# Sums of state products by accumulating DMAs: every second unit of the first level, and the second level, on one Trainium2 core

## The reference

```
xz = conv1x1(groupnorm(x)); x1, z = split(xz)            # 128 channels each
f1 = conv1x1(x1)           # 32x32 = 1024 positions      (level 1)
f2 = conv2x2_stride2(f1)   # 16x16 =  256 positions      (level 2)
f3 = conv2x2_stride2(f2)   #  8x8  =   64 positions      (level 3)

def ssm(x, ...):           # x: 128 channels, L positions, 16 states
    delta = softplus(...); B, C = projections of x       # B, C: L x 16
    h[n, t] = h[n, t-1] * exp(delta[t] * A[n]) + delta[t] * B[t, n] * x[t]
    y[t] = sum over n of h[n, t] * C[t, n]  +  x[t] * D
    return layernorm(y) over the channels

y3 = ssm(f3) + backward ssm(f3);  y2 = ssm(f2) + backward ssm(f2) + up2(y3)
y1 = ssm(f1) + backward ssm(f1) + up2(y2)
x  = x + conv1x1(y1 * silu(z))
```

## Time and profile before

| | |
|---|---|
| median of three runs | 4344.43 us |
| profiled execution | 4338.19 us |
| its span | 4336.4 us |
| DVE busy | 3559.6 us, 82% |
| POOL busy | 3338.1 us, 77% |
| PE busy | 3086.1 us, 71% |
| ACT busy | 2552.1 us, 59% |
| load queue's share of the 16 DMA engines | 45.0% |
| mean granted clock of TensorE | 0.825 of full |

### The profile page before, as it was taken

How to read it: one execution, slowest core, us unless ns; L and a number is a source line. 1 busy time by engine, 2 the same in 40 slices (tenths; PEclk the granted TensorE clock), 3 DMA queues, 4 the chain that set the end, 5 groups by cost and what they waited for, 6 DMA issues and landing times.

```text
span 4336.4 us, 51200 instructions
## 1 busy us (share of the span) xinstructions
PE 3086.1 (71%) x11852; PEld 1449.5 (33%) x11852; DVE 3559.6 (82%) x4199; ACT 2552.1 (59%) x6006; POOL 3338.1 (77%) x1908
## 2 busy tenths in 40 slices
PE   6977767777776778767777876777877777876511
PEld 3433333333332433333333333333333333332200
DVE  2178888888888888888888888888888888898777
ACT  4466665655665665666656666665676566565432
POOL 0069597895969879696896969789596996969798
PEclk8988788888888888887888888888887888888755
DMA  1036354463544446354453534446253454635444
GB/s 40 1 125 206 117 179 147 157 200 108 197 140 157 165 147 204 115 190 146 157 186 125 201 129 167 149 159 209 99 196 131 168 174 137 205 113 182 165 157 174
DMA packets 187260, 663.95 MB, mean 153 GB/s; under 512 B 22736, under 2 KB 24672, under 8 KB 186976
## 3 DMA queue, kind: packets, MB, share of 16 engines
q1 hardware_dynamic: 186976, 661.47, 45.0%
HBM read 639.76 MB, written 21.63 MB: 153 GB/s over the span
## 4 chain that ended last, share of the span: by engine, by line
POOL 28%; issue 23%; DVE 17%; PE 13%; ACT 11%; DMA 6%; DVEq 1%; POOLq 1%; SPq 0%; ACTq 0%
POOL bx L1342 12%; POOL y L1370 7%; DMA bb<-bc_rows 6%; DVE h L581 6%; POOL h L1365 5%; ACT diag L1085 5%; PE pconv L822 4%; DVE slot_c L572 3%; POOL bx L1345 2%; PE pm L848 2%; DVE rs L528 1%; DVE rs L520 1%; ACT slot_b L1200 1%; PE pm L839 1%; POOL delta L1310 1%
## 5 line engine op out<-in xcount | busy, mean ns | idle before, releaser
L822 PE MATMUL pconv<-pad,diag 128*128 128x512 f16 x8064 | 2052.6, 412 | 132.7 <-DVE xn L506 66.9
L1370 POOL TENSOR_TENSOR y<-y,h 128x1024 f32<-128x1024 f32 (+2 forms) x672 | 1335.6, 1987 | 153.9 <-DVE h L581 131.2
L1200 ACT ACTIVATE slot_b<-delta,nega 128x512 f32<-128x512 f32 (+1 forms) x1280 | 804.3, 640 | 1010.6 <-DVE slot_c L572 1009.0
L822 PEld LDWEIGHTS pconv<-pad,diag 128*128 128x128 f16 x8064 | 826.1, 104 | 1328.6 <-issue 423.3
L1342 POOL TENSOR_TENSOR bx<-bb,u 128x1024 f32<-128x1024 f32 x512 | 1219.4, 2382 | 19.9 <-DMA bb<-bc_rows 19.9
L572 DVE TENSOR_TENSOR_SCAN slot_c<-slot_b,bx 128x512 f32<-128x512 f32 (+1 forms) x1024 | 954.2, 956 | 296.1 <-POOL bx L1342 255.4
L581 DVE TENSOR_TENSOR h<-slot_c,cb 128x512 f32<-128x512 f32 x1280 | 860.4, 673 | 36.6 <-POOL y L1370 36.6
L572 DVE TENSOR_TENSOR_SCAN slot_c<-slot_b,slot_c,bx 128x512 f32<-128x512 f32 x512 | 663.7, 1296 | 74.8 <-ACT slot_b L1200 18.7
L1310 POOL TENSOR_TENSOR delta<-delta,rs 128x512 f32<-128x512 f32 (+1 forms) x96 | 111.8, 1164 | 464.6 <-DVE rs L530 464.6
L1365 POOL TENSOR_TENSOR h<-h 128x512 f32<-128x512 f32 (+3 forms) x384 | 361.2, 941 | 98.3 <-DVE h L551 80.7
L1085 ACT ACTIVATE diag<-id,chi 128x128 f16<-128x128 f16 x1344 | 426.6, 386 | 10.7 <-PE pconv L822 10.1
(11 more groups left out here) (168 smaller groups left out, 3555.2 us busy)
## 6 DMA issues: line engine op xcount, KB each, us to landing
bb<-bc_rows SPq DMA_DIRECT2D x592, 512.0 KB, 4.5
cb<-bc_rows SPq DMA_DIRECT2D x592, 512.0 KB, 4.4
xr<-in_x SPq DMA_DIRECT2D x16, 1024.0 KB, 4.9
out<-ob SPq DMA_DIRECT2D x16, 1024.0 KB
bc_rows<-rows SPq DMA_DIRECT2D x64, 64.0 KB, 1.6
w<-in_w SPq DMA_DIRECT2D x2, 256.0 KB
wc<-in_wc SPq DMA_DIRECT2D x2, 256.0 KB
bc_rows<-rows SPq DMA_DIRECT2D x16, 32.0 KB, 1.5
```

The lines of the kernel that those rows point to most:

```text
L822: ins = nc.tensor.matmul(bank(pconv, k), w, pad[:, t, part, rows:rows + 16, dx:dx + W], start=first and m == 0, stop=last and m == 2)
L1200: ins = nc.scalar.activation(slot_b[:, o:o + w], delta[:, so + c:so + c + w], ACT.Exp, scale=nega[:, st, n0 + n:n0 + n + 1])
L1370: pool.tensor_tensor(yv, yv, src[:, 0] if len(src.shape) == 3 else src, ALU.add).then_inc(q_y.sem, 1)
```

## The change

`ob`, idle until the end of an image, becomes a second accumulator, one [128 x 1024] array a direction, and DMAs that POOL issues and that add into their destination take over a part of POOL's adds.

- **Level 2** (`flat`). The products of the first level-2 unit (`rounds(q) == 0`) are written by DVE straight into `ob[:, d]` and not into the ring; for this DVE's wait for the last image's store (`ob_free`) moves from `output` to this weighing. The products of units 2 to 4 are written to the ring and added whole (1024 wide, four states side by side) to `ob[:, d]` by an accumulating DMA, six an image. It waits for the DMA of the same direction before it (semaphore `q_flat`). In POOL's step 6 (`FOLD_AT`), behind `bx` of unit 7 and ahead of the add of unit 5's product, `fold` halves `ob[:, d]` twice and adds it to `y`, once for each direction.
- **Level 1** (`by_dma`). The products of the states 1, 3, ..., 15 of each direction are no longer added by POOL. The first of each direction is copied to `ob[:, d]` by a DMA, the seven others are added to it by accumulating DMAs. Each waits for the one before it (semaphore `q_acc`).
- **The ring.** The weighing of product q waits for the landing of product q - 3's DMA where that has one, for nothing where it went straight to `ob`, else as before for POOL's add.
- **Centring.** For norms 2 to 5 the sum stands in two places, so `norm_centre` runs two matmuls into the same bank, one of `y` and one of `ob`. It waits for `q_acc` too.

```
+def by_dma(q):
+    u, _ = PRODUCTS[q]
+    return UNITS[u][0] == 1 and UNITS[u][3] % 2 == 1
+def flat(q):
+    u, _ = PRODUCTS[q]
+    return UNITS[u][0] == 2
+def rounds(q):
+    return UNITS[PRODUCTS[q][0]][3] // 4
...
             def weigh(i, q, p):
+                if flat(q) and rounds(q) == 0:
+                    if p == 0:
+                        dve.wait_ge(ob_free.sem, ob_free.at(i + 1, 0))
+                    nc.vector.tensor_tensor(half(ob[:, PRODUCTS[q][1]], b), bank(slot_c, b), half(cb[:, k % CR], b),
+                                            ALU.mult).then_inc(q_pr.sem, 1)
+                    return
                 if p == 0 and q >= HR:
-                    dve.wait_ge(q_y.sem, q_y.at(i, q - HR + 1))
+                    if flat(q - HR):
+                        if rounds(q - HR):
+                            d = PRODUCTS[q - HR][1]
+                            dve.wait_ge(q_flat[d].sem, q_flat[d].at(i, 16 * rounds(q - HR)))
+                    elif by_dma(q - HR):
+                        dve.wait_ge(q_acc.sem, q_acc.at(i, 16 * sent(q - HR + 1)))
+                    else:
+                        dve.wait_ge(q_y.sem, q_y.at(i, added(q - HR + 1)))
...
             def norm_centre(i, k):
+                pe.wait_ge(q_acc.sem, q_acc.at(i, 16 * sent(NORM_NEEDS[k])))
+                nc.tensor.matmul(o, cen[:, :], src, start=True, stop=False)
+                nc.tensor.matmul(o, cen[:, :], ob[:, d, c0:c0 + n], start=False, stop=True).then_inc(n_yc.sem, 1)
...
+            def fold(i, d):
+                q = next(v for v in range(NP) if folded(v) and PRODUCTS[v][1] == d)
+                m, n, c0 = 4, L2, L1
+                src = ob[:, d, :].rearrange("p (m l) -> p m l", m=m)
+                pool.wait_ge(q_flat[d].sem, q_flat[d].at(i, 16 * rounds(q)))
+                halve(i, src, m)
+                pool.wait_ge(q_y.sem, q_y.at(i, added(q)))
+                pool.tensor_tensor(y[:, d, c0:c0 + n], y[:, d, c0:c0 + n], src[:, 0], ALU.add).then_inc(q_y.sem, 1)
...
             def gather(i, q):
+                if by_dma(q):
+                    pool.wait_ge(q_pr.sem, q_pr.at(i, weighed(q)))
...
+                        pool.wait_ge(q_acc.sem, q_acc.at(i, 16 * sent(q)))
+                        pool.sem_inc(pool_held, 1)
+                        if UNITS[k][3] == 1:
+                            pool.dma_start(ob[:, d, :], h[:, q % HR, 0:ln]).then_inc(q_acc.sem, 16)
+                        else:
+                            pool.dma_start(ob[:, d, :], h[:, q % HR, 0:ln], accum_op=ALU.add).then_inc(q_acc.sem, 16)
+                    return
...
+                if flat(q):
+                    if rounds(q):
+                        if rounds(q) > 1:
+                            pool.wait_ge(q_flat[d].sem, q_flat[d].at(i, 16 * (rounds(q) - 1)))
+                        pool.sem_inc(pool_held, 1)
+                        pool.dma_start(ob[:, d, :], h[:, q % HR, 0:HW], accum_op=ALU.add).then_inc(q_flat[d].sem, 16)
+                    return
...
             def unit(i, j, m, k):
                 if i is not None:
                     if k + 1 < NU:
                         inputs(i, k + 1)
+                    if k == FOLD_AT:
+                        fold(i, 0)
+                        fold(i, 1)
```

More of the change, by code:

```diff
@@ L89, in weighed, with folded, added, sent @@
     return q + 1 if q < 2 else 2 * q
+def by_dma(q):
[4 more added lines that the diff above has]
+    return UNITS[u][0] == 2
+def folded(q):
+    return flat(q) and UNITS[PRODUCTS[q][0]][3] + 4 == NS
+def rounds(q):
+    return UNITS[PRODUCTS[q][0]][3] // 4
+def added(q):
+    return sum(not by_dma(v) and (folded(v) or not flat(v)) for v in range(q))
+def sent(q):
+    return sum(by_dma(v) for v in range(q))
 NHALF = 2 * (NP - 2)
@@ L303, in build @@
         q_pr = Count("q_pr", weighed(NP - 1))
-        q_y = Count("q_y", NP)
-        n_y = Count("n_y", 24)
+        q_y = Count("q_y", added(NP))
+        q_acc = Count("q_acc", 16 * sent(NP))
+        q_flat = [Count(f"q_flat{n}", 16 * (NS // 4 - 1)) for n in range(2)]
+        n_y = Count("n_y", 12)
         n_yc = Count("n_yc", NN)
@@ L873, in norm_centre @@
                     pe.wait_ge(n_o.sem, n_o.at(i, STEPS[k]))
-                pe.wait_ge(q_y.sem, q_y.at(i, NORM_NEEDS[k]))
+                pe.wait_ge(q_y.sem, q_y.at(i, added(NORM_NEEDS[k])))
                 o = norm_psum(k)[0][:, 0:cols]
@@ L1347, in inputs, with halve @@
                 ins.then_inc(u_bx.sem, 1)
+            def halve(i, src, m):
+                while m > 1:
+                    m //= 2
+                    pool.tensor_tensor(src[:, 0:m], src[:, 0:m], src[:, m:2 * m], ALU.add).then_inc(n_y.sem, 1)
+                    gather.n += 1
+                    pool.wait_ge(n_y.sem, n_y.at(i, gather.n))
+            def fold(i, d):
[6 more added lines that the diff above has]
+                pool.tensor_tensor(y[:, d, c0:c0 + n], y[:, d, c0:c0 + n], src[:, 0], ALU.add).then_inc(q_y.sem, 1)
             def gather(i, q):
@@ L1354, in gather @@
                 yv = y[:, d, fc:fc + ln]
+                if by_dma(q):
+                    pool.wait_ge(q_pr.sem, q_pr.at(i, weighed(q)))
+                    pool.sem_inc(pool_held, 1)
+                    if sent(q) == 0:
+                        pool.wait_ge(q_y.sem, q_y.at(i, added(q)))
+                        pool.sem_inc(pool_held, 1)
+                        pool.dma_start(ob[:, d, :], h[:, q % HR, 0:ln]).then_inc(q_acc.sem, 16)
+                    else:
+                        pool.wait_ge(q_acc.sem, q_acc.at(i, 16 * sent(q)))
+                        pool.sem_inc(pool_held, 1)
+                        if UNITS[k][3] == 1:
+                            pool.dma_start(ob[:, d, :], h[:, q % HR, 0:ln]).then_inc(q_acc.sem, 16)
+                        else:
+                            pool.dma_start(ob[:, d, :], h[:, q % HR, 0:ln], accum_op=ALU.add).then_inc(q_acc.sem, 16)
+                    return
                 if q == 0:
@@ L1362, in gather @@
                     src = h[:, q % HR, 0:m * g].rearrange("p (m l) -> p m l", m=m)[:, :, 0:ln]
-                while m > 1:
-                    m //= 2
-                    pool.tensor_tensor(src[:, 0:m], src[:, 0:m], src[:, m:2 * m], ALU.add).then_inc(n_y.sem, 1)
-                    gather.n += 1
-                    pool.wait_ge(n_y.sem, n_y.at(i, gather.n))
+                halve(i, src, m)
                 if q:
-                    pool.wait_ge(q_y.sem, q_y.at(i, q))
+                    pool.wait_ge(q_y.sem, q_y.at(i, added(q)))
                 pool.tensor_tensor(yv, yv, src[:, 0] if len(src.shape) == 3 else src, ALU.add).then_inc(q_y.sem, 1)
@@ L1438 @@
            (0, L1, 0), (0, L1, HALF), (2 * NS * L1, L1, 0), (2 * NS * L1, L1, HALF)]
+FOLD_AT = 6
 CHUNKS_OF = {0: 1, 1: 2, 5: 4, 21: 6}
```

5 lines of the change are left out of this document (2 added, 3 removed).

## The result

The changed kernel takes 4469.76 us, median of four runs (4455.41 to 4478.41), against 4343.6 us for the kernel before (four runs, 4341.24 to 4347.71): a ratio of 1.0298, interval 1.0274 to 1.0322. It is slower, as forecast, and inside the range, but the loss is about 126 us where 37 were forecast. The profiled execution has a span of 4464.5 us against 4336.4.

The account below looks back on a forecast made before the run. No engine was taken as full: the bound changes along an image, with DVE waiting for POOL in places and PE pacing the bridge. 16 x (2.7 + 2.0 - 2.4) = +37 us gave a median of 4381 us, range 4250 to 4530.

Parts of the forecast that it names:

- term A: Bridge between images: the doubled centring of norms 4 and 5 on PE is hidden by nothing, +2.7 us an image.
- Term B: Level 2 and the fold: what POOL saves there is spent waiting and folding, +2.0 us an image.
- the walk: Level 2 of one image followed in time, with issues of 1.0 us and landings of 5 us: unit 10 starts 2.0 us later.
- Term C: Units 18 to 30: a pair of units takes 8.85 us for 9.24, limited by DMA contention, -2.4 us an image.
- R2: Rival: slow accumulations, landings of 8 us, DMA engines the bound, level-2 weighings and fold wait; +182 us, 4526 us, chance 0.18.
- R1: Rival: DMA engines have room and the issue is short, so DVE bounds the tail; -88 us, 4256 us, chance 0.28.
- R3: Rival: each DMA issue occupies POOL as long as the add did, 2.3 us; +147 us, 4491 us, chance 0.12.
- the new waits for a DMA: Sign the forecast is right: DVE's weighing or POOL's bx newly waits for a DMA; no size given.
- the wait above 5 us at unit 8: Sign the forecast is right: DVE waits 5 us or more at unit 8, behind the fold.
- two centring pairs for each: Sign the forecast is right: two centring pairs each for slot_b and slot_c, and the bridge longer by 2 to 3 us.
- DMA share above 85%: Sign the forecast is right: the DMA engines' share in the tail rises above 85%.

Follow-up runs that it names:

- e2: Changed kernel with level 1 back to adds on POOL and one centring matmul, so only the level-2 DMAs stay: 4495.82 us, ratio 1.0376.
- e1: Changed kernel with level 2 back to gathers on POOL, so only the level-1 DMAs and the second centring stay: 4349.98 us, ratio 1.0040.
- e6: Changed kernel with four ring buffers for the products instead of three: 4374.65 us, ratio 1.0090.
- e3: Changed kernel with all DMAs as plain copies, the addition left out, so the output is not the reference's: 4306.77 us, ratio 0.9935.
- e7: Changed kernel with three buffers for the loads of bb instead of two: 4352.16 us, ratio 1.0041.
- e10: Changed kernel with only the level-1 DMAs (level 2 gathered by POOL), three bb buffers and four ring buffers: 4227.02 us, ratio 0.9735.
- e4: Changed kernel without the second centring matmul of norms 2 to 5, so the output is not the reference's: 4450.95 us, ratio 1.0273.
- e5: Changed kernel with the two folds one POOL step later, behind bx of unit 8 and the add of unit 5's product: 4433.32 us, ratio 1.0228.
- e11: Whole changed kernel with the folds one step later, four ring buffers and three bb buffers: 4252.67 us, ratio 0.9794.
- e12: Kernel before, without POOL's DMAs, given three bb buffers and four ring buffers: 4351.73 us, ratio 1.0035.

## Why the prediction was right in sign and wrong in size

The sign held: POOL's relief is spent on level 2. It did not hold by much. With term A as measured (1.3) and the other two as forecast, the sum would have been 0.9 us an image or 14 us, near the 9 us that the forecast couldn't tell from no change. Of the three terms one failed, one was twice too large, and two places that the sum put at nothing were not nothing.

**Term B, level 2 and the fold, is the step that failed:** +2.0 us an image forecast, +7.1 measured (+1.7 in u1 to u5, +5.4 in u5 to u10). What was mis-sized is the landing, 5 us from the end of the issue, "just over the load, which is the row nearest in size". The first slot came 6.9 us after the start of the issue where the walk had 6.0, so the forecast's 0.9 us of delay became 1.7. The walk then said "Later level-2 slots land in time" and had the fold start 5.0 us after the end of an issue. The landing measured there is 9.4 us from the issue's start, 8.5 from its end, so that the weighing of unit 6 waits 3.8 us and the scan of unit 8 waits 7.06 for its bx. With landings of 8 us the same walk gave about +7. e2 shows the term alone (+8.9 us, whole period +9.6), e1 that it vanishes with level 2 (-1.3 us), and e6 that a fourth slot takes away the waits at the ring (202.9 us to 7.8) and leaves the fold's.

The nearest row was the wrong guide for two reasons. It is a load landing among loads with the engines 66.1% busy, whereas the accumulation that the fold waits for lands beside another of its kind and four loads; and an accumulation takes 2.31 us of the engines where a load takes 1.55. Issued into empty queues it lands in 4.5 us. e3 splits the two in part: without the addition u1 to u10 is 70.3 us against 74.8, still 2.7 above before.

**Term C, the tail:** -2.4 forecast, -2.2 measured, and 1.5 loads per accumulation was right. (The working has 2.5 for 6.5 pairs; units 18 to 30 are six pairs, which gives 2.3.) That DMA time alone bounds the stretch is not so: the same transfers are 93% of units 18 to 30 in the changed kernel and 98% in e7, where the stretch is 2.7 us shorter. The rest was the loads of bb, which two buffers let start too late, as the forecast also said. POOL did not bind it: its issue takes 0.62 us from start to start for the 1.0 of the forecast, so its pair needs 7.6 us and not 7.9, where 9.1 were paid.

**What the sum put at nothing.** The forecast held that a landing on level 1 fits before its slot is needed, "2.35 + 1 + 5 = 8.35 us". It does not always: from unit 10 on DVE waits 3.7 us an image for landings at its weighings (0.8 in u10 to u18, 2.0 in the tail, 0.9 behind unit 30), and in e1, with level 1 alone, 3.4. Behind unit 30 this is the loss of 1.1 us, since with four ring buffers (e6, e10) that stretch is 41.91 or 41.92 us again. In u10 to u18 the loss is 0.5 us; both the third bb (e7, 1.9 us shorter) and the fourth slot (e6, 1.3) take back more than that. The forecast had said that "Loads have only two buffers for bb" and applied it to the tail alone.

**Term A, the bridge:** +2.7 forecast, 1.2 in PE's rows of 13 images, 1.3 in e4. The centring block runs 1.8 us longer in the mean (5.07 for 3.31), and what follows it runs 0.5 us shorter. The forecast took one added pair at the clock of the earlier trace rows for the centring and the other above it. In the image shown the clock rose within the block, so the last pair took 1.02 us, and the matmuls behind it, at a mean granted clock of 1.00 for 0.95, gained too. Over all runs the nine kernels with four pairs take 15.8 us from the first centring to the output matmuls and the five with two 14.1.

**The rivals.** R2 had the right number for level 2 (+7) and the wrong point of decision. It put it at a pair's DMA time above 9.24 us in the tail, and four loads and an accumulation take 8.5. Its other sign, accumulations landing after 8 us, was there in four of the six of level 2 (medians 8.8, 8.3, 9.3 and 11.1 us, the others 6.9 and 4.6). The landing time and the engines' time are two sizes; the transfers were slow to land without the tail being lost. Its +182 us lies above the +126 measured chiefly by its terms for the tail (+1.7 for -2.2 us an image) and the bridge. R1 is excluded by the accumulations' 2.31 us, R3 by the issue of 0.62 us.

**What would show it.** Seen: the new waits for a DMA, the wait above 5 us at unit 8, two centring pairs for each, DMA share above 85%. DVE's waits for bx in units 18 to 30 fell from 7.1 to 2.6 us an image, by more than the third forecast, and 2.0 us came back as waits at the ring. Not seen: the bridge is longer by 1.2 us and not by 2 to 3, and POOL's busy time fell by 565 and not 890 us. The profile does count POOL's own DMA issues as busy, 299 us of them, although it doesn't count those of SP.

**The experiments' own misses.** e2 cost 41 us more than expected: without the DMAs of level 1, POOL's backlog behind the fold lasts longer. e3 was expected at 4390 us and took 4306.77, since the expectation looked at u1 to u10 and more than half of what the addition costs lies behind it. e5 returned 2.5 us for 4.7: the fold displaces the next bx wherever it stands while POOL has a backlog. e7 returned far more than expected (118 us for 50), since the third buffer had been counted behind unit 10 only. e6 (4374.65 for 4415), e10 (0.9735 for 0.981) and e11 (0.9794 for 0.985) did better than expected and lie outside their ranges, although e11's u1 to u10, 67.4 us, is near the branch that kept level 2's landings on the path (68) and not near 65. e12, expected at 0.992 to 1.000, is 1.0035; its stages in the table are as expected, and the excess lies in the bridge's column, which no run explains.
